# Smaller first transfer, a first pair masked and folded on its own, 512-wide routed down products, and PSUM tiles of their own for the last down products

## What is computed

```python
# L0: one 128x128 matrix for each batch
w_bot = einsum('bg,got->bot', y, weight * mask)
x = x + einsum('bnt,bot->bno', x, w_bot) + bias
# L1: base product and a LoRA of rank 16, experts weighted by cond_8
x = x + x @ W_base.T + b_base + lora * 2
# L2: gelu MLP 128 -> 512 -> 128; the two best of 8 experts for each batch, weighted, and a shared one
x = x + sum_e dense_w[b, e] * mlp_e(x) + mlp_shared(x)
# L3: silu MLP 128 -> 256 -> 128 with biases, one expert for each batch
hidden = silu(x @ wu + bu) * (x @ wg + bg)
x = x + hidden @ wd + bd
```

## Time and profile before

| | |
|---|---|
| median of 3 runs | 140.63 us (140.25 to 141.07) |
| profiled execution, own time | 141.52 us |
| its span, first to last instruction | 139.6 us |
| PE busy | 134.1 us (96%) |
| DVE, ACT, POOL busy | 99.6, 98.6, 74.0 us |
| granted TensorE clock over the span | 1.000 |

### The profile page before, as it was taken

How to read it: one execution, slowest core, us unless ns; L and a number is a source line. 1 busy time by engine, 2 the same in 40 slices (tenths; PEclk the granted TensorE clock), 3 DMA queues, 4 the chain that set the end, 5 groups by cost and what they waited for, 6 DMA issues and landing times.

```text
span 139.6 us, 3278 instructions
## 1 busy us (share of the span) xinstructions
PE 134.1 (96%) x930; PEld 125.0 (90%) x930; DVE 99.6 (71%) x191; ACT 98.6 (71%) x203; POOL 74.0 (53%) x87
## 2 busy tenths in 40 slices
PE   6999999999999999999999999999999999999980
PEld 5988888888888889999999999999999999999870
DVE  0687998796757658577686775866858667788790
ACT  3595697979964658877779777575675669877840
POOL 0258159766990054386584965844534434444540
PEclk9999999999999999999999999999999999999999
DMA  5999999996003966565575564765656656654124
GB/s 148 349 406 408 408 403 401 380 379 258 0 0 129 377 247 257 224 276 238 220 303 236 228 252 195 293 268 225 252 201 272 271 236 246 263 218 167 38 78 152
DMA packets 11202, 34.56 MB, mean 248 GB/s; under 512 B 1072, under 2 KB 2096, under 8 KB 11184
## 3 DMA queue, kind: packets, MB, share of 16 engines
q1 hardware_dynamic: 11184, 34.34, 62.7%
HBM read 12.32 MB, written 1.05 MB: 96 GB/s over the span
## 4 chain that ended last, share of the span: by engine, by line
PE 93%; DVE 2%; issue 1%; ACT 1%; ACTq 0%
PE up L287 32%; PE acc L287 31%; PE gate L287 30%; DVE x_res L942 1%; DVE h_lo L977 0%; ACT h_act L655 0%; ACT h_hi L593 0%; ACTq L215 0%; DVE slabs L786 0%; DVE up L968 0%; ACT out_part L634 0%; ACTq L611 0%; DVE shift_pick L787 0%; ACT dn_hi L611 0%; ACTq L592 0%
## 5 line engine op out<-in xcount | busy, mean ns | idle before, releaser
L725 POOL TENSOR_TENSOR dn_lo<-slabs,dn_hi 128x256 fp32r<-128x256 f32 x40 | 29.6, 741 | 42.9 <-ACT dn_hi L611 42.9
L587 ACT ACTIVATE h_act<-gate 128x512 f32<-128x512 f32 x48 | 28.8, 599 | 27.2 <-PE gate L287 25.8
L880 DVE SCALAR_TENSOR_TENSOR up<-h_act,w_route,up 128x512 f32<-128x512 f32 x32 | 24.2, 755 | 20.9 <-PE up L287 20.9
L870 DVE TENSOR_TENSOR h_lo<-up,h_hi 128x512 fp32r<-128x512 f32 x55 | 37.5, 683 | 0.4 <-ACT h_hi L593 0.4
L287 PE MATMUL gate<-x_hi,w_gu 128*128 128x256 f32 x160 | 35.6, 283 | 0.3 <-ACT h_act L655 0.2
L287 PE MATMUL up<-x_hi,w_gu 128*128 128x256 f32 x160 | 35.4, 281 | 0.0
L593 ACT ACTIVATE h_hi<-up 128x512 fp32r<-128x512 f32 x55 | 32.8, 596 | 0.0
L287 PEld LDWEIGHTS gate<-x_hi,w_gu 128*128 128x128 f32 x160 | 27.6, 189 | 1.0 <-issue 0.9
L287 PEld LDWEIGHTS up<-x_hi,w_gu 128*128 128x128 f32 x160 | 27.7, 189 | 0.0
L287 PE MATMUL up<-x_lo,w_gu 128*128 128x256 f32 x80 | 22.6, 283 | 0.0
L287 PE MATMUL gate<-x_lo,w_gu 128*128 128x256 f32 x80 | 22.6, 283 | 0.0
(11 more groups left out here) (116 smaller groups left out, 214.8 us busy)
## 6 DMA issues: line engine op xcount, KB each, us to landing
w_gu<-slabs SPq DMA_DIRECT2D x40, 512.0 KB, 3.0
slabs<-slabs_moe SPq DMA_DIRECT2D x8, 768.0 KB, 13.0
slabs<-slabs_l SPq DMA_DIRECT2D x4, 768.0 KB, 8.0
outT<-x_res SPq DMA_DIRECT2D x8, 128.0 KB, 2.0
sh_raw<-slabs_shared SPq DMA_DIRECT2D x2, 384.0 KB, 5.6
x_res<-x_rest SPq DMA_DIRECT2D x1, 768.0 KB, 7.2
slabs<-second_in SPq DMA_DIRECT2D x1, 384.0 KB, 4.0
cond_all<-first_in SPq DMA_DIRECT2D x1, 381.0 KB, 3.0
```

The costliest lines, as they stand in the source:

```text
L587: nc.scalar.activation(h_act[:, u % 2, :], gate_ps[u % 2][:], ACT.Gelu_apprx_tanh).then_inc(act_done, 1)
L725: nc.gpsimd.tensor_tensor(dn_lo[:, q % W_SLOTS, :], slab_cols(at, DOWN_AT, 256), dn_hi[:, q % W_SLOTS, :].bitcast(F32), ALU.subtract).then ...
L870: V.tensor_tensor(h_lo[:, u % H_SLOTS, :], h_of(u), h_hi[:, u % H_SLOTS, :].bitcast(F32), ALU.subtract).then_inc(h_lo_done, 1)
L880: ins = V.scalar_tensor_tensor(h_of(u), h_act[:, k, :], weight, h_of(u), ALU.mult, ALU.mult)
```

## The change

- **Transfers.** `first_in` shrinks from 762 to 506 columns; the constants come in four transfers in place of three (506, 640, 512, 384 columns, the same total of 2042). Blocks 0 and 1 of `w_l0` come with the first, 2 to 5 with the second, 6 and 7 and the mask with the third; the base matrix and the identity with the fourth.
- **Warm-up.** The last of the three matmuls on zeros is 128 wide in place of 256.
- **First pair.** Batches 0 and 1 are masked, added and folded one by one (`first_matrix`), and the mask of the other six follows.
- **ACT.** `round_shared(0)` moves behind the second exponential and the gelu table load.
- **Routed down products.** `h_hi` and `h_lo` lie side by side in `h_pair`. `both` multiplies `dn_hi` with both at once, 512 columns wide, into a whole bank; DVE adds its two halves one after the other (`add_halves`).
- **L3 end.** Down products 4 to 7 get PSUM tiles of their own; the last up half goes into the second half of acc's bank 1. Batches 0, 1, 2 and 4 go through ACT and POOL, 3, 5, 6 and 7 are finished by DVE. ACT itself sends batch 4.

```diff
-WARM_UP = 3
+WARM_UP = (256, 256, 128)
...
-POOL_SUMS = range(2, 4)
-
-OUT_GROUPS = ((0, 1), (1, 2), (2, 3), (4, 5), (3, 4), (5, 6), (6, 7), (7, 8))
+POOL_SUMS = (0, 1, 2, 4)
+FINISHED = (3, 5, 6, 7)
...
-C_COLS = C_W + 4 * P
-
-
-def build(nc, x_first, first_in, second_in, third_in, x_rest, slabs_moe, slabs_l3, slabs_shared, outT):
+C_COLS = C_W + 2 * P
...
-        second_sb = early(6, P)
+        second_sb = early(5, P)
         third_sb = early(4, P)
-        zeros = early(S)
+        fourth_sb = early(3, P)
+        zeros = early(P)
...
-        h_hi = sb("h_hi", [P, H_SLOTS, 512], F32R)
-        h_lo = sb("h_lo", [P, H_SLOTS, 512], F32R)
+        h_pair = sb("h_pair", [P, H_SLOTS, 2, 512], F32R)
+        h_hi, h_lo = h_pair[:, :, 0, :], h_pair[:, :, 1, :]
...
-        last_up = [up_ps[1][:, 0:S], up_ps[3][:, 0:S]]
-        m_banks = [gate_ps[0][:, 0:S], gate_ps[1][:, 0:S], up_ps[1][:, 0:S], acc_ps[:, S:2 * S]]
-
-        d_first, d_second, d_third, d_x, d_x_rest = (
-            sem(n) for n in ("d_first", "d_second", "d_third", "d_x", "d_x_rest"))
+        last_up = [up_ps[1][:, 0:S], acc_ps[:, 512 + S:1024]]
+        m_first_banks = [up_ps[0][:, 0:P], gate_ps[0][:, 0:P]]
+        m_banks = [None, gate_ps[1][:, 0:S], up_ps[1][:, 0:S], acc_ps[:, S:2 * S]]
...
-            return (acc(0, S), acc(1, S), up_ps[2][:, 0:S])[t % 3]
+            return (acc(0, S), acc(1, S), up_ps[2][:, 0:S], acc(0, S), up_ps[3][:, 0:S], gate_ps[1][:, 0:S],
+                    gate_ps[0][:, 0:S], up_ps[0][:, 0:S])[t]
...
+            sp.dma_start(fourth_sb[:, :, :], fourth_in).then_inc(d_fourth, DMA)
...
-            for first_b, after_b in OUT_GROUPS:
-                last_b = after_b - 1
-                if last_b in POOL_SUMS:
-                    sp.wait_ge(summed, last_b - POOL_SUMS[0] + 1)
+            for t in (0, 1, 2, 3, 5, 6, 7):
+                if t in POOL_SUMS:
+                    sp.wait_ge(summed, POOL_SUMS.index(t) + 1)
                 else:
-                    sp.wait_ge(acc_read, ACC_BIAS + PAIRS + B + last_b + 1)
-                at = slice(first_b * S, after_b * S)
+                    sp.wait_ge(finished, FINISHED.index(t) + 1)
+                at = slice(t * S, (t + 1) * S)
                 sp.dma_start(outT[:, at], x_res[:, at]).then_inc(d_out, DMA)
-            sp.wait_ge(d_out, len(OUT_GROUPS) * DMA)
+            sp.wait_ge(d_out, B * DMA)
...
-            for _ in range(WARM_UP):
-                mm(acc_ps[:, 0:S], zeros[:, 0:P], zeros[:], True, True)
-
-
-            for k in range(2):
-                pe.wait_ge((d_first, d_second)[k], DMA)
-                for i in range(4):
-                    last = mm(up_ps[2 + k][:, i * P:(i + 1) * P], w_l0_parts[k][:, i, :], y_diag, True, True)
-                last.then_inc(w0_sum, 1)
-            pe.wait_ge(d_third, DMA)
+            for n in WARM_UP:
+                mm(acc_ps[:, 0:n], zeros[:], zeros[:, 0:1].to_broadcast([P, n]), True, True)
+
+
+            for k in range(TBLK):
+                if k == 0:
+                    pe.wait_ge(d_first, DMA)
+                elif k == 2:
+                    pe.wait_ge(d_second, DMA)
+                elif k == 6:
+                    pe.wait_ge(d_third, DMA)
+                block_sum = mm(up_ps[2 + k // 4][:, (k % 4) * P:(k % 4 + 1) * P], w_l0_blocks[k], y_diag, True, True)
+                if k % 4 == 3:
+                    block_sum.then_inc(w0_sum, 1)
...
+            pe.wait_ge(d_fourth, DMA)
...
+            def first_matrix():
+
+                pe.wait_ge(w0_ready, 2)
+                for b in range(2):
+                    pe.wait_ge(r1_first, b + 1)
+                    mm(m_first_banks[b], w0_b[:, b, :], r1_b[:, b, :], True, True).then_inc(m_first_sum, 1)
+
             def matrix(p):
 
-                pe.wait_ge(r1_ready, (1, 3, 3, 3)[p])
-                pe.wait_ge(w0_ready, 2)
+                pe.wait_ge(r1_ready, 2)
+                pe.wait_ge(w0_ready, 4)
...
-                pe.wait_ge(m_ready, 1)
+                pe.wait_ge(w0_ready, 4)
                 for b in range(2):
+                    pe.wait_ge(m_first, b + 1)
...
-                slab_down(R0 + q, q, acc(b, S), j == 0, j == 3)
+                hidden_split(R0 + q)
+                pe.wait_ge(wd_hi_done, q + 1)
+                pe.wait_ge(wd_lo_done, q + 1)
+                slot = (R0 + q) % H_SLOTS
+
+                def both(c, start, stop):
+                    w, h = slice(c * P, (c + 1) * P), slice(c * S, (c + 1) * S)
+                    return mm(acc(b, 512), dn_hi[:, q % W_SLOTS, w], h_pair[:, slot, :, h], start, stop)
+
+                def low(c):
+                    w, h = slice(c * P, (c + 1) * P), slice(c * S, (c + 1) * S)
+                    mm(acc(b, S), dn_lo[:, q % W_SLOTS, w], h_hi[:, slot, h], False, False)
+
+                both(0, j == 0, False)
+                low(0)
+                low(1)
+                both(1, False, j == 3).then_inc(down_done, 1)
...
-                elif t >= 3:
-                    pe.wait_ge(acc_read, ACC_BIAS + PAIRS + B + t - 2)
+                elif t == 3:
+                    pe.wait_ge(biased, 1)
+                elif t == 4:
+                    pe.wait_ge(h_lo_done, T0 + 6)
+                else:
+                    pe.wait_ge(act_done, T0 + 2 * (B - 1) + t - 4)
...
-                        pe.wait_ge(h_lo_done, T0 + t - 1)
+                        pe.wait_ge(biased, 2)
...
-            round_shared(0)
...
+            round_shared(0)
...
+                if t >= 4:
+                    add_bias(t - 4)
...
+            add_bias(4)
+            act.wait_ge(summed, len(POOL_SUMS))
+            act.dma_start(outT[:, 4 * S:5 * S], x_res[:, 4 * S:5 * S]).then_inc(d_out, DMA)
...
+                if 4 <= q - UNITS_ROUTED < B - 1:
+                    add_residual(q - UNITS_ROUTED - 4)
+            add_residual(4)
...
-            mask_w0(0)
+            mask_w0(0, 0, 2)
...
+            dve.wait_ge(lora_sum, 1)
+            for b in range(2):
+                V.tensor_tensor(r1_b[:, b, :], gate_ps[0][:, b * P:(b + 1) * P], base_i[:], ALU.add).then_inc(r1_first, 1)
             dve.wait_ge(a_bias_sum, 1)
             V.tensor_tensor(a_bias_y[:], acc_ps[:, 512:512 + B], cond_scaled[:], ALU.mult).then_inc(a_bias_ready, 1)
+            mask_w0(0, 2, 6)
+            dve.wait_ge(r1_first, 2)
+            for b in range(2):
+                dve.wait_ge(m_first_sum, b + 1)
+                V.tensor_tensor(m_b[:, b, :], m_first_banks[b], r1_b[:, b, :], ALU.add).then_inc(m_first, 1)
+            mask_w0(1, 2, 6)
             add_base(1, 2, 4, gate_ps[1][:])
-            dve.wait_ge(r1_ready, 1)
-            combine(0)
+            dve.wait_ge(c_sum, 1)
+            V.tensor_scalar(c_b[:], acc_ps[:, 0:B], bias_l1, None, ALU.add).then_inc(acc_read, ACC_BIAS)
...
+            def add_halves(b, down):
+
+                at = slice(b * S, (b + 1) * S)
+                dve.wait_ge(down_done, down)
+                V.tensor_tensor(x_res[:, at], acc(b, 512)[:, S:2 * S], x_res[:, at], ALU.add).then_inc(half_added, 1)
+                dve.wait_ge(half_added, b + 1)
+                V.tensor_tensor(x_res[:, at], acc(b, S), x_res[:, at], ALU.add).then_inc(acc_read, 1)
...
+                        add_halves(b - 1, R0 + 4 * b)
...
+            finish(3)```

The order on PE in the routed stage, from the end of an up product to the end of the down product behind it. Before:

```order
L287 MATMUL up2<-x_hi,w_gu 128x256
L287 MATMUL acc<-h_hi,dn_hi 128x256
L287 MATMUL acc<-h_lo,dn_hi 128x256
L287 MATMUL acc<-h_hi,dn_lo 128x256
L287 MATMUL acc<-h_hi,dn_hi 128x256
```

More of the change, by code:

```diff
@@ L327, in matrix @@
                 last.then_inc(m_sum, 1)
-            matrix(0)
+            first_matrix()
             pe.wait_ge(bw_ready, 3)
@@ L955, in _ @@
                 if t == ACC_AT:
-                    add_acc(B - 1, S, T0)
+                    add_halves(B - 1, T0)
                 if t == ACC_AT + 1:
                     round_x3(B - 1)
-                if 4 <= t < 4 + POOL_SUMS[0]:
-                    finish(t - 4)
+            finish(3)
             t = B - 1
@@ L993, in cond_layout @@
     c[:, C_VECS:C_W] = vecs
-    c[:, C_W:] = w_l0.reshape(P, 4 * P)
+    c[:, C_W:] = w_l0.reshape(P, 2 * P)
     return c
@@ L1029 @@
     data = {
-        "x_first": xT[:, 0:PAIR], "x_rest": xT[:, PAIR:], "first_in": cond_layout(a(cond_8), vecs, w_l0[:, 0:4]),
-        "second_in": second, "third_in": third,
+        "x_first": xT[:, 0:PAIR], "x_rest": xT[:, PAIR:], "first_in": cond_layout(a(cond_8), vecs, w_l0[:, 0:2]),
+        "second_in": second, "third_in": third, "fourth_in": fourth,
         "slabs_moe": slabs_moe, "slabs_l3": slabs_l3, "slabs_shared": slabs_shared.reshape(P, HALVES, SLAB).transpose(1, 0, 2),
```

74 lines of the change are left out of this document (35 added, 39 removed).

## The result

The changed kernel takes 139.06 us (median of 22 runs, 138.35 to 140.48) against 140.69 us for the kernel before on the same chip (22 runs, 139.71 to 142.46). The ratio is 0.9886, 95% interval 0.9861 to 0.9911: 1.6 us faster, which is clear of noise. The profiled execution took 138.68 us, with a span of 136.9 us.

A forecast was written before the change was run, and what follows sets the result against it. PE, busy 96% of the span, was taken as the bound. Gains of 0.38 + 0 + 0.39 + 0.9 = 1.67 us, subtracted from the 140.63 us median, gave 139.0 us; range 138.3 to 140.1, leaving 2 in 10 out.

The forecast's parts named there:

- Wide products: Routed down products: each of 64 merged pairs saves 5.9 ns, 0.38 us in all, kept as 0 to 0.38.
- Front: Start up to the first shared product: PE's earlier start is mostly lost; sum 0, between -0.3 and +0.4 us.
- DVE's last mask step decides when `first_x2` starts: Front: first_x2 waits for DVE's 384-column mask step, until 9.8 us, and its first product starts at 9.87.
- a gap of over 0.3 us there: Front: a PE gap at first_x2 or matrix over 0.3 us would show the forecast wrong.
- The steps of DVE behind it: Front: 512-wide addition, c_b and 256-wide addition, 0.60 + 0.13 + 0.42 us, to 10.9; PE's next matrix waits.
- My band for the first shared product: End of the front: first shared product at 11.5 to 12.1 us, as a sign of being right.
- Rival 4: Front: the clock rises 4.7 us later, at 11.4 us, costing 2.35 us; 141.4 us, chance 0.06.
- End of L3: Last unit's second half: PE's wait for unit T0+5's h_lo goes, 0.39 us.
- Behind PE: Outputs after PE's last product: SP issues the last one right behind finish; 1.08 us less, taken as 0.9.
- The change removes 128 instructions, so the block never comes: PE's queue: without 64 matmuls and 64 weight loads the program ends before the last instruction packet; 7 packets, not 8.
- Rival 2: Output issue stays slow for another reason; gain 0.77 us, 139.9 us, chance 0.22.
- 255 records between two packets: PE's instruction fetch: 255 records, with waits some 270 instructions, lie between packets, so packets follow PE's count.

The follow-up runs named there:

- front_free: Kernel after with narrower waits ahead of first_x2 and matrix(1), and DVE rounding x_hi ahead of the second choice's reduction; 139.05 us, ratio 0.9883.
- before_pad: Kernel before with three already passed semaphore waits added to PE in each of 32 routed units, no work added; 140.12 us, ratio 0.9983.
- after_pad: Kernel after with four or five already passed waits added to PE in each routed unit, no work added; 139.8 us, ratio 0.9945.
- before_again: Kernel before, unchanged, measured against itself for a second profile; 140.71 us, ratio 0.9978.
- wide alone: Kernel before with only h_pair, 512-wide routed down products and add_halves, measured twice; 140.0 us, ratio 0.9972, and 139.35 us, ratio 0.9918.
- tail alone: Kernel before with only the new L3 end: own tiles, new engine shares, ACT sending batch 4; 139.61 us, ratio 0.9947.
- front alone: Kernel before with only the new front: four transfers, shorter warm-up, first pair folded on its own; 140.42 us, ratio 0.9978.
- after_again: Kernel after, unchanged, measured once more for a second profile; 138.99 us, ratio 0.988.
- narrow_after: Kernel after with routed down products narrow again, six 256-column matmuls a unit, and add_acc; 139.84 us, ratio 0.9971.

## Why the prediction was right

It forecast 139.0 us and the kernel takes 139.06. That the two agree within 0.1 us is partly luck: the interval of the ratio allows 1.25 to 1.96 us of gain, and the four terms were off by 0.07 to 0.15 us in both directions. Term by term, with sizes from the table:

- **Wide products, 0.38 us.** The direction is right, the size is off: 32 x 16.6 ns = 0.53 us ((2.1532 - 2.1366) a unit). The step that failed is the use of 119.6 ns, the mean of a unit, for each 256-wide matmul, with the others left unchanged. "233.3 ns each" was nearly right: from start to start a wide product takes 234.2 ns (mean of 50 in the kernel after), and four narrow ones on `dn_hi` took 475.0 ns together in before. So the merges themselves save 6.6 ns a unit, where 11.8 was forecast. The other 10 ns come from matmuls that were not merged: the two on `dn_lo` take 4 ns less together, the twelve gate and up products 6 ns. All eight profiles with wide products show this split within 1 ns; why the neighbours go faster is not shown. That the two runs of 256 columns lie apart costs nothing that can be seen. DVE's added halves are hidden: its groups rose from 99.6 to 102.2 us busy, and PE doesn't wait for them. By the formula for an isolated matmul in the Trainium skill ("TensorE: Matmul & The Clock Gate", Back-to-back issue gap) a merge would be worth an estimated 2.5 ns. The runs show 3.3 for the pair itself and 8.2 with its neighbours.
- **Front, 0.** Right against the one profile of before, and nearly right for the profiles as they are (0.07 us); at equal turns it is a gain of some 0.2 us, because the old front often has a wait that the profile of before lacks. By the prediction's steps DVE's last mask step decides when `first_x2` starts. It does, and costs PE the 0.32 us that front_free takes away: a gap of over 0.3 us there was one of the listed signs of being wrong, and the forecast held in spite of it. The steps of DVE behind it, 9.87 + 1.15 us, end at 11.0 and not at 10.9 as the prediction has it; no term hangs on this. My band for the first shared product, 11.5 to 12.1 us, missed its 11.33, since I took the turn at 6.7 us for fixed. It came between 4.3 and 7.3 us in 14 executions, and each us of it moves the start by 0.46 us. Rival 4, a turn near 11 us, did not come: it is at 5.3 to 7.3 us with the new front and at 4.3 to 6.9 with the old.
- **End of L3, 0.39 us.** The stall of 0.385 us is gone wherever the new tiles are. The last unit takes 0.48 us less in all. The other 0.1 us are two short delays behind the stall in before, which the prediction left out: the record behind the late gate product starts after 0.20 us in place of 0.12, and one in the last down product after 0.15.
- **Behind PE, 0.9 us.** Cause right, as far as profiles show it: before_pad changed no work, moved the packets, and the long issue went. The size in profiles: tails of 4.27, 3.87 and 4.17 us, mean 4.10, became 3.29, so 0.81 us. Without a long issue the old order has 3.17; the new one is 0.12 us slower (I had set aside 0.18 for outputs that come close together). "The change removes 128 instructions, so the block never comes" is right (7 packets in all eight profiles with wide products), but it is not the only way: with the new L3 end alone the last packet came at 130.9 us and did no harm. Rival 2, an issue that stays slow, did not come: with wide products none took over 0.44 us. The sentence of the Trainium skill ("Runtime: NRT & Kernel Launch", Instruction fetch mechanics) that a crossing is mostly hidden agrees with PE's own pace: in the kernel after, units with a packet in them take 2.13 to 2.14 us like the rest. For other queues it does not hold here: an issue on SP's queue took 1.61 us in place of 0.44, and PE lost 1.3 us by a late copy in after_pad. The prediction's 255 records between two packets are no proof of blocks of 256. The profile has 183 to 293 of them from packet to packet, and of waits it records only a part, so it neither confirms nor refutes that size.

The profiles' terms make 0.53 + 0.07 + 0.48 + 0.81 = 1.89 us, the medians 1.63. The interval of the ratio holds both. What stays open is the long issue's worth in an average run. Profiles say 0.8 to 1.1 us; before_pad, which removes nothing else, won 0.65 us by its medians and 0.24 by its ratio, and before_again has 0.3 by its ratio with no change at all. The parts (by their ratios: wide alone 0.4 and 1.2 us, tail alone 0.7, front alone 0.3) don't add up to 1.6 us. They need not, since wide products and L3 end each remove the same long issue, and with an uncertainty of 0.4 to 0.5 us each they can't test the terms. The sizes of the four terms rest on profiles.

What was not foreseen at all is the wait at q = 2. It is missing from the profile after, which accounts for 0.24 us of the 2.7 by which the two spans differ, and is back in after_again. The turn, 1.2 us sooner, would account for some 0.55 us more by the line.

## What to carry to other kernels

When the last output is issued long after its data are ready, look for an instruction packet in the DMA queues at that moment, and try to move it by changing the number of instructions of the longest stream. A few passed waits may be enough, but where the packets went was foreseen roughly in one such test here (before_pad) and not in the other (after_pad). Split a wait on "all steps" into the step whose bank or rows the next instruction touches. Compare stages over several profiles before a difference between two is believed: here the turn alone, between 5.3 and 7.1 us, moved the first shared product of one and the same front by 0.8 us.

## What the runs showed of the hardware

- A fetch of PE instructions (one packet of 16 KB, 0.9 to 1.7 us) goes with an issue on SP's queue that ends 0.4 us after it (three of three profiles with a packet at 134.2 to 134.9 us; with the packets moved, in before_pad, it is gone). It left another issue at 0.33 us (narrow_after). A copy of 512 KB that was issued in the usual 0.49 us landed 1.4 us late beside one (after_pad), and 64 of the 66 slowest copies in 14 profiles had one beside them.
- Passed waits added to PE cost its pace nothing: the routed unit takes 2.1536 and 2.1368 us with them, 2.1532 to 2.1536 and 2.1364 to 2.1368 without. Only 64 of 96, and 72 of 136, appear as instructions.
- PE's pace doubles (f32 records of 128 columns 0.21, then 0.11 us apart: the clock's lower level, 1.2 GHz, and 2.4 GHz) at 4.3 us in one execution of the kernel before and at 6.7 in another, with the same first start of PE, 1.17 us. Over all 14 profiles it is 4.3 to 7.3 us.
- A 512-wide matmul takes 234.2 ns from start to start in a routed unit. The 14 matmuls of 256 columns beside two of them take 119.2 ns each; in the unit without 512-wide ones the same 14 take 119.9.
